# Explicit opening and closing lists, a new steady order, v in 512-byte rows and twelve groups of zero matmuls

## What is computed

```
scale, shift = split(cond @ W_emb + b_emb)
xn  = rms_norm(x) * g_norm * (1 + scale) + shift
q, k, v = split(xn @ W_qkv)                     # 16 heads of 16
q, k = rms_norm(q) * g_q, rms_norm(k) * g_k
o   = softmax(q k^T / 4) v                      # inside each sequence
h0  = o + o @ W_out                             # "r" below
h   = rms_norm(h0)
att = causal_attention(h * ln1; Wq, Wk, Wv) @ Wo
mod = 0.1 * tanh(att @ A)
gate = silu(h * ln2 @ W_in^T + mod * (h * ln2 @ A) @ B)
out = x + h0 + (gate * (h * ln2 @ W_up^T)) @ W_down^T
```

## Time and profile before

| | us |
|---|---|
| median of three runs | 675.9 |
| lowest and highest | 675.0, 676.04 |
| the profiled execution | 674.3 |
| its span, first to last instruction | 672.5 |
| PE busy, share of the span | 599.9, 89% |
| DVE busy | 461.7, 69% |
| ACT busy | 368.7, 55% |
| POOL busy | 218.4, 32% |

### The profile page before, as it was taken

How to read it: one execution, slowest core, us unless ns; L and a number is a source line. 1 busy time by engine, 2 the same in 40 slices (tenths; PEclk the granted TensorE clock), 3 DMA queues, 4 the chain that set the end, 5 groups by cost and what they waited for, 6 DMA issues and landing times.

```text
span 672.5 us, 22378 instructions
## 1 busy us (share of the span) xinstructions
PE 599.9 (89%) x9056; PEld 553.0 (82%) x9056; DVE 461.7 (69%) x1074; ACT 368.7 (55%) x770; POOL 218.4 (32%) x196
## 2 busy tenths in 40 slices
PE   2345569999999999999999999999999999997987
PEld 2334459998998989998999899998998899996887
DVE  3465867778686777777786867686777778684532
ACT  2354537565565748374656657483747466562412
POOL 0121132515143433425151524334251506141213
PEclk9755979999999999999999999999999999998989
DMA  5142010111101010111011010101111110101000
GB/s 155 48 153 68 21 40 2 35 32 34 34 18 50 12 55 9 27 34 32 33 33 33 18 49 14 53 9 27 35 31 32 34 32 19 34 15 35 8 26 17
DMA packets 40151, 24.32 MB, mean 36 GB/s; under 512 B 24016, under 2 KB 38992, under 8 KB 40064
## 3 DMA queue, kind: packets, MB, share of 16 engines
q1 hardware_dynamic: 40064, 23.02, 12.4%
HBM read 14.61 MB, written 4.19 MB: 28 GB/s over the span
## 4 chain that ended last, share of the span: by engine, by line
PE 66%; SPq 14%; DVE 7%; ACT 4%; DMA 4%; issue 3%; POOL 1%; POOLq 0%; ACTq 0%; DVEq 0%
SPq L338 14%; PE gate_bank L387 11%; PE up_bank L387 9%; PE b_banks L387 7%; PE down_bank L581 7%; PE a_banks L379 7%; PE x_bank L379 5%; PE b_banks L379 4%; PE a_banks L472 4%; PE b_banks L399 2%; DMA vj<-vs 2%; PE gate_bank L567 2%; PE b_banks L534 2%; PE a_banks L399 2%; PE x_bank L490 1%
## 5 line engine op out<-in xcount | busy, mean ns | idle before, releaser
L979 POOL TENSOR_TENSOR qk<-qk,rx 128x512 f32<-128x512 f32 x32 | 34.3, 1092 | 229.4 <-DVE rx L783 229.4
L991 POOL TENSOR_TENSOR gl<-gu,gh 128x512 fp32r<-128x512 f32 x64 | 81.6, 1285 | 70.5 <-ACT gh L735 70.5
L387 PE MATMUL up_bank<-uh,wup_hi 128*128 128x256 f32 x256 | 78.7, 307 | 0.7 <-DVE gu L885 0.7
L387 PE MATMUL gate_bank<-uh,win_hi 128*128 128x256 f32 x256 | 75.0, 293 | 0.3
L387 PE MATMUL up_bank<-ul,wup_hi 128*128 128x256 f32 x256 | 72.9, 285 | 0.0
L387 PE MATMUL up_bank<-uh,wup_lo 128*128 128x256 f32 x256 | 72.7, 284 | 0.0
L581 PE MATMUL down_bank<-wdn_hi,gh 128*128 128x256 f32 x256 | 71.9, 281 | 0.7 <-POOL gl L991 0.7
L581 PE MATMUL down_bank<-wdn_hi,gl 128*128 128x256 f32 x256 | 72.1, 282 | 0.0
L581 PE MATMUL down_bank<-wdn_lo,gh 128*128 128x256 f32 x256 | 72.0, 281 | 0.0
L387 PE MATMUL gate_bank<-ul,win_hi 128*128 128x256 f32 x256 | 71.7, 280 | 0.0
L387 PE MATMUL gate_bank<-uh,win_lo 128*128 128x256 f32 x256 | 71.6, 280 | 0.0
(11 more groups left out here) (153 smaller groups left out, 1811.7 us busy)
## 6 DMA issues: line engine op xcount, KB each, us to landing
xa<-in_x SPq DMA_DIRECT2D x16, 256.0 KB, 2.8
xres<-in_x SPq DMA_DIRECT2D x16, 256.0 KB, 2.9
vj<-vs SPq DMA_DIRECT2D x256, 16.0 KB, 1.8
out<-outb SPq DMA_DIRECT2D x16, 256.0 KB, 3.2
stage<-in_w_inT SPq DMA_DIRECT2D x2, 512.0 KB, 4.0
stage<-in_w_upT SPq DMA_DIRECT2D x2, 512.0 KB, 3.7
stage<-in_w_downT SPq DMA_DIRECT2D x2, 512.0 KB, 4.0
stage<-in_w_qkv SPq DMA_DIRECT2D x2, 384.0 KB, 3.7
```

Source lines behind the costliest of these rows:

```text
L387: mm = pe.matmul(dst, w[a][:, k, c0:c0 + P], mov[b][:, k, :], start=(first and k == 0 and j == 0), stop=(last and k == KT - 1 and j == 2), ...
L979: pool.tensor_tensor(heads_of, heads_of, rx[:, 32 * t:32 * t + 32].unsqueeze(2).to_broadcast([P, 2 * H, HD]), ALU.mult).then_inc(done[name ...
L991: pool.tensor_tensor(gl[:, c % 2], gu[:, c % 2], gh[:, c % 2].bitcast(F32), ALU.subtract).then_inc(f_lo, 1)
```

## The change

It replaces the shifted walk of one list by three lists, and changes four things beside.

1. `START` (an explicit list of steps with block numbers, weight steps and loads among them), then ten periods of a new `ORDER` for periods 4 to 13, then `END` (explicit). `WEIGHTS_AT`, `period` and the `weights` functions go; their work becomes steps `load`, `hi`, `lo`, `own`, `mblk`, `m_mm`, `v2_mm`, `v2_hi`, `v2_lo`, `masks`, `g_col`, `head_masks` and the like. Each small load has a semaphore of its own.
2. `w_emb` and `condT` are issued by ACT (`ld_emb`), and the embedding products are two steps, `emb_scale` and `emb_shift`.
3. `vs2` becomes [128, 4, 2, 64] and h @ A goes to a tensor `ha` by a second ACT copy, so each of the 16 DMAs moves 32 partitions of 512 contiguous bytes, before 2 x 256.
4. Piece `b` is cast by one ACT operation on 96 rows with a mask as scale; the three casts and the memset of `b3` go. `cT` and `mblk` lie in other tensors' memory.
5. `warm`: three matmuls of `mt` (zeros) into `Ub[0:96, 0:192]`. It stands twelve times in `START`.

The other steps keep their bodies. SP's first steps are `ld_heads`, `load` 0, `x_load` 0, `x_load` 1, `ld_ln`, `ld_ident`, `ld_wv`, `load` 1, `ld_b_emb`, `x_load` 2, `ld_wo_a`, `ld_g`, `load` 2. The core of the diff:

```diff
 ORDER = [
+    ("x_load", 2), ("x_norm1", 1), ("f_half2", -2), ("b_v_out1", -1), ("a_turn1", 0), ("b_shift1", -1),
+    ("f_hi1", -2), ("b_move", -1), ("a_turn0", 0), ("f_up2", -2), ("a_k_out0", 0), ("f_lo1", -2), ("b_shift0", -1),
...
+LOOP_FROM, LOOP_TO = 4, 14
+START = [
+    ("mt_zero", 0), ("ld_emb", 0), ("first_rms", 0), ("b_emb_one", 0), ("warm", 0), ("warm", 0), ("warm", 0),
+    ("warm", 0), ("warm", 0), ("emb_scale", 0), ("scale_cols", 0), ("emb_shift", 0), ("ld_heads", 0), ("load", 0),
...
+        def run(eng, do, looped=True):
+            for name, n in START:
+                do(name, n, n % 2)
...
-        vs2 = sb("vs2", [P, TB, D + R])
-        vj = sb("vj", [P, TB, 4, 4 * R])
+        vs2 = sb("vs2", [P, 4, TB, 4 * R])
+        ha = sb("ha", [P, TB, R])
+        vj = sb("vj", [P, 4, TB, 4 * R])
...
-                            sp.dma_start(vj[32 * j:32 * j + 32, :, b, :],
-                                         vs2[32 * b:32 * b + 32, :, 4 * R * u:4 * R * u + 4 * R]).then_inc(v_moved, 16)
+                            sp.dma_start(vj[32 * j:32 * j + 32, b].rearrange("p t r -> p (t r)"),
+                                         vs2[32 * b:32 * b + 32, u].rearrange("p t r -> p (t r)")).then_inc(v_moved, 16)
...
+                elif name == "warm":
+                    pe.wait_ge(once["mt_zero"], 1)
+                    for _ in range(3):
+                        pe.matmul(Ub[0:96, 0:192], mt[:, 0, :], mt[:, :, :].rearrange("p t n -> p (t n)"), start=True, stop=True)
...
-                    act.activation(vs2[:, t, :], Xb[:, 0:D + R], ACT.Copy).then_inc(done[name], 1)
+                    act.activation(vs2[:, :, t, :], Xb[:, 0:D].rearrange("p (u r) -> p u r", u=4), ACT.Copy)
+                    act.activation(ha[:, t, :], Xb[:, D:D + R], ACT.Copy).then_inc(done[name], 1)
```

More of the change, by code:

```diff
@@ L35 @@
 ORDER = [
[L36 to L39, removed]
[14 rows of a table removed]
-]
-FIRST = -max(s for _, s in ORDER)
-LAST = NB - 1 - min(s for _, s in ORDER)
@@ L59 @@
-LOOP_FROM = 2 * ((3 - min(s for _, s in ORDER)) // 2)
-LOOP_TO = LOOP_FROM + 2 * ((NB + FIRST - LOOP_FROM) // 2)
-SHIFT = dict(ORDER)
-X_BANK_READER = {"x_turn": "x_scale", "a_v": "a_v_out", "r_turn": "r_lo", "b_v0": "b_v_out0", "b_v1": "b_v_out1"}
-X_BANK_ORDER = [name for name, _ in ORDER if name in X_BANK_READER]
[9 rows of a table added]
+    ("a_flip0", 0), ("m_mul", -1), ("a_pv0", 0), ("a_pv1", 0), ("x_scale", 1), ("m_turn", -1), ("x_shift", 1),
+    ("o_odd", 0), ("m_out", -1), ("o_even", 0), ("f_down3", -2), ("o_hi", 0), ("f_gate0", -1), ("x_hi", 1),
[7 rows of a table added]
+]
@@ new lines @@
+END = [
[9 rows of a table added]
+    ("a_weigh0", 14), ("x_shift", 15), ("x_hi", 15), ("o_odd", 14), ("o_hi", 14), ("f_half0", 13), ("f_hi3", 12),
[3 rows of a table added]
+    ("m_tanh", 13), ("r_mm", 14), ("m_turn", 13), ("a_copy1", 15), ("f_lo3", 12), ("m_out", 13), ("a_scale0", 15),
[5 rows of a table added]
+    ("b_move", 13), ("r_load", 14), ("a_scores", 15), ("b_q", 14), ("b_v1", 14), ("f_up1", 13), ("f_gate2", 13),
[6 rows of a table added]
+    ("b_pv", 14), ("f_down1", 13), ("r_mm", 15), ("f_down2", 13), ("m_turn", 14), ("r_load", 15), ("m_mul", 14),
+    ("r_rms", 15), ("f_out", 13), ("f_down3", 13), ("r_lo", 15), ("r_add", 15), ("f_up0", 14), ("o_hi", 15),
[12 rows of a table added]
+    ("f_out", 14), ("m_tanh", 15), ("f_hi3", 14), ("f_mul1", 15), ("f_store", 15), ("m_out", 15), ("f_tanh0", 15),
[4 rows of a table added]
+]
@@ L67 @@
+X_BANK_READERS = {"x_turn": ["x_scale"], "a_v": ["a_v_out"], "r_turn": ["r_lo"],
+                  "b_v0": ["b_v_out0"], "b_v1": ["b_v_out1"]}
 PIECES = [("qkv0", 768), ("qkv1", 768), ("w_out", 512), ("q2", 512), ("k2", 512), ("a2", 32),
@@ L160, in bass_adaln_attention_ffn @@
         Db = ctx.enter_context(nc.psum_tensor("down_bank", [P, 512], F32))
-        done = {name: sem(name) for name, _ in ORDER if name[:2] != "f_" and name[2:] not in ("load", "move")}
+        done = {name: sem(name) for name, _ in ORDER if name[:2] != "f_" and name[2:] != "load" and name != "b_move"}
         f_up, f_gate, f_tanh, f_half, f_mul, f_hi, f_lo, f_down, f_out = (
@@ L196, in wait_dma @@
                 eng.wait_ge(s, 8 * n + (8 if odd else 16))
+        steady = [(name, p + shift) for p in range(LOOP_FROM, LOOP_TO) for name, shift in ORDER]
+        x_bank_uses = [(name, n) for name, n in START + steady + END if name in X_BANK_READERS]
         def wait_x_bank(pe, name, n):
-            p = n - SHIFT[name]
-            i = X_BANK_ORDER.index(name)
-            for back in range(1, 2 * len(X_BANK_ORDER)):
-                turns, j = divmod(i - back, len(X_BANK_ORDER))
-                before = X_BANK_ORDER[j]
-                m = p + turns + SHIFT[before]
-                if not isinstance(n, int) or 0 <= m < NB:
-                    wait(pe, done[X_BANK_READER[before]], m)
-                    return
@@ L210, in period @@
[L210 to L222 removed]
+            i = x_bank_uses.index((name, n))
@@ L223, in run @@
+            if i > 0:
+                before, m = x_bank_uses[i - 1]
+                for reader in X_BANK_READERS[before]:
+                    wait(pe, done[reader], m)
+        def run(eng, do, looped=True):
+            for name, n in START:
+                do(name, n, n % 2)
             if looped:
                 with eng.Fori(LOOP_FROM, LOOP_TO - 1, 2) as p:
[L225 to L229 removed]
```

388 lines of the change are left out of this document (213 added, 175 removed), and 112 rows, old and new, of tables (END, ORDER, START).

## The result

| | before | after |
|---|---|---|
| median of four runs each, us | 675.45 | 646.88 |
| lowest and highest | 674.49, 676.04 | 645.86, 651.59 |
| the profiled execution and its span | 674.3, 672.5 | 646.44, 644.6 |
| PE, DVE, ACT, POOL busy, us | 599.9, 461.7, 368.7, 218.4 | 600.9, 462.1, 370.0, 221.1 |

The ratio of the runs is 0.9592 with an interval of 0.9543 to 0.9641: faster by 4.1%. The forecast was 647.0, 633 to 662. PE does the same products as before and 72 passes of zeros more, which take 14.7 us (7.42 + 2.11 + 3.09 + 2.11 in its timeline). So the products themselves are busy for some 14 us less: about 6 before `r_mm`(1), 4 from there to `r_mm`(14) and 3 behind it. The rest of the gain is shorter gaps. One run of after stands 5 us above the other three, at a mean clock of 0.962 against 0.973 and 0.974; the experiments come back to that.

What follows compares the result with a forecast made beforehand. PE, nearly always busy, was taken as the bound. Head -16.8, middle -3.7 and tail -8 took the span from 672.5 to 644; plus 1.8 and 1.6 made 647 us, range 633 to 662.

Steps and rivals of the forecast that it cites:

- Head: Opening up to `r_mm`(1): earlier loads, zeros and overlapped blocks bring that milestone to 83.5 us, minus 16.8.
- The walk: Opening costed step by step from operation durations: `a_qk0`(0) near 17.5, `r_mm`(0) about 49, `r_mm`(1) 82, taken as 83.5.
- The loop: Steady periods: 35.9 us each, bounded by 35.6 and 37.3; the 0.66 loss a period mostly the move of v.
- the price of a copy: Move of v in the loop: 512-byte rows issue in 0.43 us, not 0.60; whole move 9.3 us, 2.8 under its slot.
- rival (a): Loop: the move of v stays at 0.60 an issue, 12.9 us in 12.1; plus 5 to 10, 654; chance 0.15.
- From `r_mm`(1) to the loop: Pipeline filling after the opening: plus 1.8 us for `f_gate0`(0) and 5 for fill loss.
- Tail: From `r_mm`(14) to the end: closing list fills gaps with the previous block's `f` work; 87 us, minus 8.
- (b): Loop: `a_pv0` waits for flips because DVE's chain starts late; plus 10 to 15 us, 659; chance 0.12.
- (c): Opening gains half, SP's queue feeding the pieces late: `r_mm`(1) at 92, total 655 us; chance 0.15.
- (e): Slower: DVE's chain between `a_scores` and `a_flip0` misses by over 2.8 us every period; 682 at 3.5; chance 0.03.
- (f): Opening: the zeros do not raise the clock, first products still slow; plus 4 us, 651; chance 0.06.
- (d): More gain: PE holds its clock in the opening and the fill costs nothing; 635 us; chance 0.09.

Runs made afterwards that it cites:

- the control: The kernel after, unchanged, measured again on one chip beside later experiments: 650.13 us, ratio to before 0.9641.
- `END` walked: The kernel after with its explicit closing list replaced by a plain walk of the new steady order: 656.43 us, ratio 0.9731.

## Why the prediction was right, and where it wasn't

**Head.** Predicted 16.8 us less at `r_mm`(1), measured 17.6 in the profile of after and 15.1 in the control's. The walk held at most steps: first product 8.5 for 8.37, `x_turn` 13.2 for 12.11, `a_qk`(0) 17.5 for 17.49, `a_pv`(0) 42 to 43 for 39.76, `r_mm`(0) 49 for 48.03, `b_k`(0) 60 for 59.93, `a_pv`(1) 75 for 75.28, `r_mm`(1) 83.5 for 82.68. At one place two errors cancel: `x_turn` came 1.1 us early, and from it to `a_qk0`(0) it took 5.4 us for 4.3. The half clock that it allowed for is there, later than put: in this execution it is full until 32 us and 0.57 in the eight behind. One reading for it was off: the third and fourth slices of before, "where PE is busy a third of the time", show four and five tenths, and 17.45 us busy of 33.65 (33.60 to 67.25). The five first groups cost what was said (8.4 for "about 8.5"). That they pay for that front is what the runs don't show: five alone changed nothing. And of the 16.8 the list itself gives the most: the loads and the cast alone brought `r_mm`(1) to 97.96, and the written lists without zeros to 87.5 and 87.7.

**The loop.** The period was predicted as 35.9 and is 35.83, in the control 35.90. The size was right and the reason mostly wrong: "In the loop the loss of 0.66 a period is mostly the move of v". Of the 0.91 us less than the 36.74 of before, the waits for the move are 0.34 (4.2 and 0.8 us in ten periods). The greater part, 0.5 to 0.7, is PE's busy time at the same products, and it goes with the new order alone. That fits the fewer returns from small tiles, which the prediction put at two of 0.1 to 0.2 each; no run isolates them. The other step that failed is the price of a copy: "I take 0.43, the copy being as plain as that load: 16 x 0.47 with the gaps + 1.8 = 9.3 us, 2.8 less than the slot". One issue costs 0.59, the move 12.5 (11.30 on the queue, of which the last issue of 0.6 lies under the 1.8 to landing) and not 9.3, and the rows alone are worth nothing that can be told (0.9978). That is the mechanism of rival (a), also the rule of the Trainium skill; only its price, 5 to 10 us, didn't come. It went by "12.9 us in a slot of 12.1". The slot is 12.6, and the issues take from 10.5 to 11.6 us in the ten periods, the move thus 11.7 to 12.8, so that it just fits: waits of 0.8 us in all, three of them, in ten periods, and up to 2.6 in the other executions of this order. The rows don't explain the saved wait of before, and the slot can't be shown to: where PE doesn't wait it is 12.5 us in the new order and 12.1 in the old one, but the old order with the new loads and the same 12.1 waited only 0.2 us for the move in its loop, since its issues took 10.5 to 11.1 us, where every second move of before took 11.2 to 12.0. Why the moves of before run long is open. Yet that kernel's period was still 36.44: waits for the move are not what keeps the old order from 35.8. The large load, a copy from HBM on 128 partitions, was the wrong row to be nearest to; the copy itself stood there at 0.60.

**From `r_mm`(1) to the loop.** Three periods and 6.8 us (1.8 for `f_gate0`(0), 5 of fill) were predicted; they take 117.07, which is 9.6 above 3 x 35.83. With the 1.8 taken off, the fill is 7.8, not 5. PE's waits there are 5.7 us (117.07 less 111.38 busy), among them 1.9 for `tok` and 1.7 for `o`; the rest is in products slower than in the loop (busy 111.38 for 3 x 35.5 + 1.8 = 108.3). Thus the middle gave 1.8 us where 3.7 stood.

**Tail.** 87 was predicted, 86.6 measured; `END` walked takes 93.4. "The 2.6 go" for `r_turn`(15): they went. "1.5 to 2 stay" for `b_pv`(15): nothing stayed. Two waits that the prediction didn't name are there instead, 1.4 at `r_turn`(14) and 0.8 at `b_pv`(14).

**The rivals.** (b): there is no wait of note for `pTa` in the loop, one of 0.2. (c) is out by `r_mm`(1). (e) is out by the period. (f) is out as it was put, since the products behind the zeros run at twice the speed; but the five groups in front bring no time, and all twelve 3 us in the median. (d), 635 with the clock held throughout, was tried in part: with the clock at 0.92 before `r_mm`(1), 645.0. In that opening PE still waits 3.5 us for the move of v, 2.6 for `pTa`, 1.9 for `al` and 1.9 for `qk`, so chains on SP's queue, DVE and POOL hold it too.

**The sum.** The terms as written give 644 + 1.8 + 1.6 = 647.4, put down as 647. That it met 646.88 is luck in part: the same kernel measured again gave 650.13, and the errors cancel. Head and tail gained 0.8 and 0.5 us more than forecast, the middle 1.9 less, and the median stands 2.3 above the profiled span, where 3.4 were added.
